# Attention scores of a cross-attention and FFN block: eight kept weight tables in place of a product per batch

## Chip, cores and metric

One core of a Trainium2 chip runs the kernel. The metric is the device time in microseconds; the time before is the median of three runs.

## What is computed

For each of 32 batches, with x and a context c of 256 rows and 512 columns:

```
q = layernorm(x)
t, p, g = Wt c, Wp q, Wg c                     (256 x 512 each)
score[G] = 0.125 * sum over group G's 32 rows and all columns of p * g      (8 groups)
u = Wz[G] (score[G] * t[G]);  normalised over each group, * gamma + beta, + c
x1 = x + that
out = x1 + FFN(layernorm(x1)),  gate/up 512 -> 1408, silu(gate) * up, down 1408 -> 512
```

The three linear layers of the FFN round their inputs and weights to FP4 (E2M1) in blocks of 16 with a scale each. The score of a group is linear in the matrix c q' (256 x 256, here called the gram matrix): it is the sum over all its elements of gram times the table Wg[G]' Wp[G].

## The kernel before

A batch is two tiles of 128 rows (t = 2b and 2b + 1; j counts tiles). The FFN weights are quantised, turned and split into two fp16 parts once at the start; they stay in SBUF. Each engine has its own list of steps, written out by hand, with semaphores between them; the first two batches are interleaved with the weight work, and then a loop `body(i)` runs for i = 1 to 30 (the last one unrolled). In body i the FFN of tiles j = 2i and j + 1 runs, beside the attention of batch i + 1 and the loading and normalising of batch i + 2.

TensorE's order in a body: `gram(i + 1)` (24 fp16 products of 256 columns, line 500), three hidden groups of tile j (`hidden`, line 550: two spans of 512 columns and one of 384, 24 products each, gate and up in turn), between the first and the second `mixed` (line 512: four fp32 products, Wg times gram) and `u_rows` twice (line 527: twelve F32R products of 512 columns, the context times the folded value weights), then `group_means` and `group_spread` (lines 535, 541: small fp32 products with a matrix of group means), `output(j - 1)` (line 561, 33 fp16 products), three hidden groups of tile j + 1, and `output(j)`. A hidden group may start when the `gated` step that reads its PSUM pair two groups before is done (`h_done`), and an output product when the transposed h has landed (`h_turned`).

The chain of h for a tile: ScalarE's silu (line 964), VectorE's `gated` (1409), block maxima (`h_first`, 1205), scales (`h_scales`), division (`h_y`, 1184), ScalarE's `grain_h` (915), VectorE's `h_snap_add` (1193), `h_snap_back` (1197), `h_quant` in two halves (1201), ScalarE's `h_hi` (873), VectorE's `h_lo` (1349), then SP's transposing DMA `turn_h` (422). For the odd tile j - 1 the part from `h_snap_add` on runs at the start of the next body. x has the same chain with 512 columns (`x_first`, `x_y`, `x_add`, `x_back`, `x_quant`, `x_lo`), and `turn_x`.

The scores: ScalarE's `gram_copy` (834) brings gram to SBUF, scaled by row; TensorE's `mixed` multiplies it by Wg; VectorE's `sum_pg` (1239) multiplies by Wp and sums each row; `group_means` adds the rows of a group; `copy_group` (1245) and GpSimd's `columns` go on. GpSimd also makes the low parts of the context (`ctx_lo`, 1797) and of q (`q_lo`, 1802), x + c (`add_ctx`, 1786), and the powers of -1/2 (1771). Line 1208 is VectorE's scale step; lines 1470, 1473 (VectorE) and 1848, 1856 (GpSimd) round and scale the weights at the start, and lines 597, 614 and 639 are TensorE's work there: the transposes of the weights, the row of maxima, and the folding of the value weights.

```python
            def mixed(b):
                pe.wait_ge(gram_copied, HT * b + HT)
                at_least(pe, pg_summed, HT * b)
...
            def h_snap_add(j):
                dve.wait_ge(h_grain_done, j + 1)
```

## Time and profile before

| | us |
|---|---|
| three runs: lowest, median, highest | 1741.19, 1742.09, 1744.41 |
| profiled execution: span from its first to its last instruction | 1739.4 |
| TensorE busy in the span | 1682.5 |
| VectorE busy | 1518.6 |
| ScalarE, GpSimd busy | 825.6, 707.2 |

The profile gives the span of the profiled execution and no other time of it; the span leaves out what lies before the first and after the last instruction. It is 2.7 us under the median of the runs. PE is TensorE's matmul, PEld its weight load, DVE is VectorE, ACT is ScalarE, POOL is GpSimd, SP is SyncE. A row of a timeline merges like instructions that follow one another (x8: eight of them); its time runs from the start of the first to the end of the last, and what stands in brackets is the idle time ahead of it and what ended that. Matmul records overlap: the next one starts before the end of the one ahead.

### The profile page before, as it was taken

How to read it: one execution, taken by the hardware profiler on the slowest of the kernel's cores; microseconds unless marked ns; L12 is line 12 of the kernel's file. 1: busy time of each engine (PE TensorE's matmuls, PEld its weight loads, DVE VectorE, ACT ScalarE, POOL GpSimd, SP SyncE). 2: the span in 40 equal slices, each digit the busy share in tenths (PEclk: the TensorE clock that was granted, in tenths of full speed). 3: DMA queues.
4: the chain of work that ended last, by engine and by line, in shares of the span. 5: the costliest groups of instructions: out<-in, count | busy, mean ns of one | idle time of the engine just before them, and what ended most of it. 6: DMA issues, size and time to landing. Idle time of an engine off the chain costs nothing.

```text
span 1739.4 us, 27808 instructions
## 1 busy us (share of the span) xinstructions
PE 1682.5 (97%) x8723; PEld 922.4 (53%) x8723; DVE 1518.6 (87%) x2577; ACT 825.6 (47%) x1472; POOL 707.2 (41%) x879
## 2 busy tenths in 40 slices
PE   2789999999999999999999999999999999999999
PEld 1666555555555555555555555555555555555544
DVE  8987888889888888988888898888888988888887
ACT  3656545444445454444554444454544444545322
POOL 6865333334444333444433334443333444433310
PEclk9999999999999999999999999999999999999999
DMA  8123334334344434343434434333434444333321
GB/s 257 34 43 66 88 89 105 88 91 97 78 94 91 94 87 99 89 96 79 93 89 94 98 83 106 75 87 90 104 87 92 96 81 93 91 92 87 76 52 47
DMA packets 412150, 155.86 MB, mean 90 GB/s; under 512 B 383200, under 2 KB 384480, under 8 KB 412128
## 3 DMA queue, kind: packets, MB, share of 16 engines
q1 hardware_dynamic: 396352, 125.17, 33.7%
q10 hardware_dynamic: 15776, 30.41, 5.4%
q8 instruction: 12, 0.20, 0.0%
q14 instruction: 10, 0.08, 0.0%
HBM read 43.03 MB, written 16.78 MB: 34 GB/s over the span
## 4 chain that ended last, share of the span: by engine, by line
PE 94%; DVE 2%; ACT 2%; DMA 1%; issue 1%; POOL 0%; SPq 0%; DVEq 0%; ACTq 0%
PE pairs L550 52%; PE work L561 25%; PE work L500 5%; PE work L512 3%; PE ubank L527 2%; PE work L527 2%; PE pairs L605 1%; PE pairs L500 0%; PE pairs L597 0%; DMA hT_parts<-raw 0%; DMA raw<-in_L_ffn_w_gate 0%; DVE w_rinv L1205 0%; DVE x_in L1223 0%; PE pairs L607 0%; PE pairs L580 0%
## 5 line engine op out<-in xcount | busy, mean ns | idle before, releaser
L550 PE MATMUL pairs<-w_gate_hi,xT_parts 128*128 128x512 f16 (+1 forms) x1536 | 555.4, 362 | 1.8 <-DMA xT_parts<-raw 1.5
L550 PE MATMUL pairs<-w_up_hi,xT_parts 128*128 128x512 f16 (+1 forms) x1536 | 554.7, 361 | 0.0
L561 PE MATMUL work<-w_parts,hT_parts 128*128 128x512 f16 x2079 | 458.9, 379 | 0.9 <-DMA hT_parts<-raw 0.9
L561 PEld LDWEIGHTS work<-w_parts,hT_parts 128*128 128x128 f16 x2079 | 203.5, 99 | 236.1 <-issue 1.1
L550 PE MATMUL pairs<-w_up_lo,xT_parts 128*128 128x512 f16 (+1 forms) x768 | 277.5, 361 | 0.0
L550 PE MATMUL pairs<-w_gate_lo,xT_parts 128*128 128x512 f16 (+1 forms) x768 | 277.4, 361 | 0.0
L550 PEld LDWEIGHTS pairs<-w_gate_hi,xT_parts 128*128 128x128 f16 x1536 | 152.7, 99 | 163.2 <-issue 15.1
L550 PEld LDWEIGHTS pairs<-w_up_hi,xT_parts 128*128 128x128 f16 x1536 | 150.3, 98 | 146.5
L964 ACT ACTIVATE early<-pairs,w_unit 128x512 f32<-128x512 f32 (+1 forms) x192 | 124.9, 651 | 166.3 <-PE pairs L550 166.3
L873 ACT CAST raw<-hq 128x704 f16<-128x704 f32 x126 | 98.1, 779 | 179.5 <-DVE hq L1201 178.7
L1409 DVE SCALAR_TENSOR_TENSOR h<-pairs,w_unit,early 128x512 f32<-128x512 f32 (+1 forms) x192 | 135.0, 703 | 39.9 <-ACT early L964 34.6
L915 ACT ACTIVATE wm<-h 128x1408 bf16<-128x1408 f32 (+2 forms) x65 | 87.1, 1341 | 166.5 <-DVE h L1184 166.5
L1786 POOL TENSOR_TENSOR xc<-x_in,c_in 128x512 f32<-128x512 f32 x64 | 88.8, 1387 | 176.6 <-DVE x L1258 176.6
L1835 POOL TENSOR_TENSOR ln_rs<-ln_mv,eps_col 128x1 f32<-128x1 f32 x64 | 59.2, 925 | 215.3 <-DVE ln_mv L1266 215.3
L1810 POOL TENSOR_TENSOR att<-rowst,grp 128x2 f32<-128x2 f32 x32 | 14.0, 436 | 280.6 <-DVE grp L1245 280.6
L1201 DVE SCALAR_TENSOR_TENSOR hq<-h,h_unit 128x704 f32<-128x704 f32 (+1 forms) x129 | 111.1, 882 | 5.5
L550 PEld LDWEIGHTS pairs<-w_gate_lo,xT_parts 128*128 128x128 f16 x768 | 75.1, 98 | 77.1
L550 PEld LDWEIGHTS pairs<-w_up_lo,xT_parts 128*128 128x128 f16 x768 | 75.1, 98 | 77.0
L1349 DVE TENSOR_TENSOR raw<-hq,raw 128x704 f16<-128x704 f32 x126 | 109.3, 887 | 1.6
L1205 DVE TENSOR_REDUCE h_amax<-h 128x88 f32<-128x1408 f32 (+1 forms) x66 | 104.0, 1575 | 2.2
L1184 DVE SCALAR_TENSOR_TENSOR h<-h,h_rinv 128x1408 f32<-128x1408 f32 (+1 forms) x66 | 104.1, 1577 | 0.1
L1197 DVE SCALAR_TENSOR_TENSOR h<-wm,h 128x1408 f32<-128x1408 bf16 (+2 forms) x65 | 102.7, 1580 | 1.2
(193 smaller groups left out, 2803.6 us busy)
## 6 DMA issues: line engine op xcount, KB each, us to landing
out<-raw SPq DMA_DIRECT2D x64, 256.0 KB, 2.1
c_in<-in_ctx ACTq DMA_DIRECT2D x29, 512.0 KB, 3.8
x_in<-in_x ACTq DMA_DIRECT2D x29, 512.0 KB, 5.3
raw<-in_L_ffn_w_down SPq DMA_DIRECT2D x2, 1408.0 KB, 8.9
raw<-in_L_ffn_w_gate SPq DMA_DIRECT2D x2, 1280.0 KB, 8.3
w_parts<-in_L_ffn_w_up SPq DMA_DIRECT2D x2, 1280.0 KB, 9.4
x_in<-in_x SPq DMA_DIRECT2D x3, 512.0 KB, 3.7
c_in<-in_ctx SPq DMA_DIRECT2D x3, 512.0 KB, 4.7
```

The lines of the kernel that those rows point to most:

```text
L550: mm = pe.matmul(pairs[:, pair, n, 0:b - a], xT[s][part][:, k, :], w1[n][wpart][:, k, a:b], start=(k == 0 and part == 0 and wpart == 0), s ...
L561: mm = pe.matmul(obank[:, :], hT[part][:, k, :], w2[wpart][:, k, :], start=(k == 0 and part == 0 and wpart == 0), stop=(k == KH - 1 and pa ...
L873: nc.scalar.copy(hq_parts[:, 0, a:b], hq[:, a:b]).then_inc(h_hi_done, 1)
L915: nc.scalar.activation(m, y, ACT.Abs, scale=GRAIN).then_inc(done, 1)
L964: nc.scalar.activation(silu[:, (s + c) % 2, 0:b - a], pairs[:, pair_of(j, s, c), 0, 0:b - a], ACT.Silu, scale=w_unit[:, 0:1]).then_inc(sil ...
L1184: nc.vector.scalar_tensor_tensor(out=blocks(y), in0=blocks(src), scalar=SNAP_BELOW, in1=over_block(rinv), op0=ALU.mult, op1=ALU.mult).then ...
L1197: nc.vector.scalar_tensor_tensor(out=y, in0=m, scalar=GRAIN, in1=y, op0=ALU.max, op1=ALU.subtract).then_inc(done, 1)
L1201: nc.vector.scalar_tensor_tensor(out=blocks(q_out), in0=blocks(y), scalar=-factor, in1=over_block(scale), op0=ALU.mult, op1=ALU.mult).then ...
L1205: nc.vector.tensor_reduce(dst, blocks(src), AX_X, ALU.max, apply_absolute_value=True).then_inc(done, 1)
L1349: nc.vector.tensor_tensor(hq_parts[:, 1, a:b], hq[:, a:b], hq_parts[:, 0, a:b], ALU.subtract).then_inc(h_lo_done, 1)
L1409: nc.vector.scalar_tensor_tensor(out=h[:, a:b], in0=pairs[:, pair_of(j, s, c), 1, 0:b - a], scalar=w_unit[:, 1:2], in1=silu[:, (s + c) % 2 ...
L1786: nc.gpsimd.tensor_tensor(xc[:, s, :], x_in[:, s, :], c_in[:, s, :], ALU.add).then_inc(xc_ready, 1)
```

## The change

From batch 2 on the scores no longer go through `mixed` and `sum_pg`. At the start TensorE makes the eight tables Wg[G]' Wp[G] (128 x 512 each in SBUF), ScalarE copies them out of PSUM, and they wait in DRAM until the weight work frees their place. In each body GpSimd multiplies the gram copy by tables 0 to 5 (`product`) and ScalarE sums each product's rows (`sum_product`), with a ring of three buffers; VectorE multiplies and sums tables 6 and 7 in one step each (`fold_product`). `group_means` gets a second small product with a matrix of ones, and `own_att` picks each row's group. The scores are made one body ahead: `gram(i + 2)` and `gram_copy(i + 2)` stand at the end of body i. The F32R products of `u_rows` are put one by one behind each pair of fp16 products of the hidden group (j, 0, 1) (`hidden_and_u`). `group_means` moves behind the third hidden group and `group_spread` behind `output(j - 1)`. Steps of ScalarE, VectorE, GpSimd and SP change their order in the body, and body 1 is unrolled. Cut to its core:

```diff
+AW = HT * C
+pg_low = raw[:, 0, 0:5 * AW].rearrange("p (g n) -> p g n", g=5)
+pg_high = raw[:, 2, 2 * D:2 * D + 3 * AW].rearrange("p (g n) -> p g n", g=3)
+pg_dram = nc.dram_tensor("pg_kept", [P, G, AW], F32).ap()
+w_small_row = w_small_parts[:].rearrange("p a b -> p (a b)")
+products = [wgT[:].rearrange("p a b -> p (a b)"), w_small_row[:, 0:AW], w_small_row[:, AW:2 * AW],
+            raw[:, 1, H + D:H + D + AW]]
+RING = len(products) - 1
+SPLIT = 6
+OLD = 2
 first_hm = hT_parts[:, 0].rearrange("p k n -> p (k n)").bitcast(BF16)
...
 def gram_bank(b):
-    return pairs[:, 0, 0, :] if isinstance(b, int) and b < 2 else work[:, 0, :]
+    return pairs[:, 0, 0, :] if isinstance(b, int) and b < OLD else work[:, 1, :]
 def mixed_bank(b):
-    return pairs[:, 0, 1, :] if isinstance(b, int) and b < 2 else work[:, 1, :]
+    return pairs[:, 0, 1, :]
+def pg_weights(g):
+    return pg_low[:, g] if g < 5 else pg_high[:, g - 5]
+def pg_staged(g):
+    return x1[:, g, :] if g < 4 else (h, hq)[(g - 4) // 2][:, (g % 2) * AW:(g % 2) * AW + AW]
+def pg_bank(g):
+    return (pairs[:, 0, 0, :], pairs[:, 0, 1, :], work[:, 1, :], pairs[:, 1, 1, :])[g % 4]
+def sums_before(b):
+    return SPLIT * (b - OLD)
+def folds_before(b):
+    return (G - SPLIT) * (b - OLD)
 def u_bank(b, s):
-    return gram_bank(b) if s else ubank[:, :]
...
             sp.dma_start(part, raw_dram[m][:, r, n * rest:(n + 1) * rest]).then_inc(raw_loaded[f], 16)
+    def load_pg():
+        sp.wait_ge(pg_saved, 48)
+        sp.wait_ge(w_rest_done, ALL_SETS)
+        sp.dma_start(pg_low, pg_dram[:, 0:5, :]).then_inc(pg_loaded, 16)
+        sp.dma_start(pg_high, pg_dram[:, 5:G, :]).then_inc(pg_loaded, 16)
     def turn_q(b):
...
         j = HT * i
         turn_h(j - 1)
         turn_x(j + 1, 1)
+        turn_h(j)
         if ahead:
             turn_c(i + 2)
+            turn_q(i + 2)
+        if more:
+            turn_x(j + 2, 0)
         store(j - 1, 1)
-        turn_h(j)
-        if ahead:
-            turn_q(i + 2)
-        if more:
-            turn_x(j + 2, 0)
         store(j, 0)
-    with sp.Fori(1, NB - 2) as i:
+    body(1)
...
-            at_least(pe, w_ready, b)
-            at_least(pe, rowst_ready, HT * b)
+            u_first(b)
         else:
-            pe.wait_ge(gram_copied, HT * b + HT)
+            u_second(b)
         for k in range(HT):
             for wpart, part in PARTS:
-                mm = pe.matmul(u_bank(b, s), wuT[wpart][:, k, s * P:(s + 1) * P], c_wide[part][:, k, :],
-                               start=(k == 0 and wpart == 0 and part == 0), stop=(k == HT - 1 and wpart == 1))
-        mm.then_inc(u_done, 1)
+                u_part(b, s, k, wpart, part)
+    def pg_matrix(g0):
+        for s in range(HT):
+            for g in range(g0, g0 + P // CG):
+                if s == 0 and g >= 4:
+                    pe.wait_ge(pg_copied, g - 3)
+                a = g % 4 * CG
+                mm = pe.matmul(pg_bank(g)[:, s * C:(s + 1) * C], w_nat[a:a + CG, 1, g // 4, s * P:(s + 1) * P],
+                               wp[a:a + CG, g // 4, :], start=True, stop=True)
+                if s == HT - 1:
+                    mm.then_inc(pg_in_psum, 1)
     def group_means(b):
         pe.wait_ge(u_copied, HT * b + HT)
-        pe.wait_ge(pg_summed, HT * b + HT)
         pe.wait_ge(rowst_ready, HT * b + HT)
-        pe.matmul(ubank[:, 0:6], gmean[:, :], rowst[:].rearrange("p h n -> p (h n)"), start=True,
-                  stop=True).then_inc(grp_done, 1)
+        if isinstance(b, int) and b < OLD:
+            pe.wait_ge(pg_summed, HT * b + HT)
+            pe.matmul(ubank[:, 0:6], gmean[:, :], rowst[:].rearrange("p h n -> p (h n)"), start=True,
+                      stop=True).then_inc(grp_done, 1)
+            return
+        pe.wait_ge(product_summed, sums_before(b) + SPLIT)
+        pe.wait_ge(product_folded, folds_before(b) + G - SPLIT)
+        pe.matmul(ubank[:, 0:2 * HT], gmean[:, :], rowst[:, :, 1:3], start=True, stop=True)
+        pe.matmul(ubank[:, 8:8 + G], ones_all[:, :], att_part[:, :], start=True, stop=True).then_inc(grp_done, 1)
     def group_spread(b):
         pe.wait_ge(sq_steps, 2 * b + 2)
         pe.wait_ge(grp_copied, b + 1)
+        if not isinstance(b, int) or b >= OLD:
+            pe.wait_ge(own_picked, b - OLD + 1)
         pe.matmul(ubank[:, 6:8], gmean[:, :], att[:, 1, :], start=True, stop=True).then_inc(spread_done, 1)
     def hidden(j, s, c):
...
         mm.then_inc(gu_done, 1)
+    def hidden_and_u(j, s, c, b):
+        pair = pair_of(j, s, c)
+        first, last = SPANS[c]
+        u_first(b)
+        for k in range(KD):
+            if k == KD // 2:
+                u_second(b)
+            for part, wpart in PARTS:
+                for n in range(2):
+                    mm = pe.matmul(pairs[:, pair, n, 0:last - first], xT[s][part][:, k, :],
+                                   w1[n][wpart][:, k, first:last],
+                                   start=(k == 0 and part == 0 and wpart == 0), stop=(k == KD - 1 and part == 1))
+                if k == KD - 1 and part == 1:
+                    mm.then_inc(gu_done, 1)
+                u_part(b, k // HT, k % HT, part, wpart)
     def output(j):
...
     mm.then_inc(attw_in_psum, 1)
+    pg_matrix(0)
+    pg_matrix(4)
     pe.wait_ge(ones_made, 1)
     top_of_rows(0)
     spread_top(0)
+    pe.wait_ge(pg_copied, G)
     turn_weights(0)
     turn_weights(1)
...
     output(0)
+    gram(2)
     def body(i):
         more = not isinstance(i, int) or i + 1 < NB
+        ahead = not isinstance(i, int) or i + 2 < NB
         j = HT * i
-        if more:
-            gram(i + 1)
         pe.wait_ge(x_turned, 16 * (j) + 16)
         pe.wait_ge(h_done, GROUPS * (j - 1) + 2)
         hidden(j, 0, 0)
         if more:
-            mixed(i + 1)
-            u_rows(i + 1, 0)
-            u_rows(i + 1, 1)
-        pe.wait_ge(h_done, GROUPS * (j))
-        hidden(j, 0, 1)
-        if more:
-            group_means(i + 1)
+            pe.wait_ge(h_done, GROUPS * (j))
+            hidden_and_u(j, 0, 1, i + 1)
+        if not more:
+            hidden(j, 0, 1)
         pe.wait_ge(h_done, GROUPS * (j) + 1)
         hidden(j, 0, 2)
         if more:
+            group_means(i + 1)
+        output(j - 1)
+        if more:
             group_spread(i + 1)
-        output(j - 1)
         pe.wait_ge(x_turned, 16 * (j + 1) + 16)
         pe.wait_ge(h_done, GROUPS * (j) + 2)
         hidden(j + 1, 1, 0)
...
         pe.wait_ge(h_done, GROUPS * (j + 1) + 1)
         hidden(j + 1, 1, 2)
         output(j)
-    with pe.Fori(1, NB - 2) as i:
+        if ahead:
+            gram(i + 2)
+    body(1)
+    with pe.Fori(2, NB - 2) as i:
         body(i)
     body(NB - 2)
     pe.wait_ge(x_turned, 16 * (NT - 2) + 16)
...
         act.wait_ge(c_inv_done, b + 1)
-        at_least(act, mixed_done, b)
+        if isinstance(b, int) and b <= OLD:
+            at_least(act, mixed_done, b)
+        else:
+            act.wait_ge(product_made, sums_before(b))
+            act.wait_ge(product_folded, folds_before(b))
         for s in range(HT):
             nc.scalar.activation(gram_sb[:, s, :], gram_bank(b)[:, s * C:(s + 1) * C], ACT.Identity,
                                  scale=c_norm[:, 3, s:s + 1]).then_inc(gram_copied, 1)
+    def copy_pg(g):
+        act.wait_ge(pg_in_psum, g + 1)
+        nc.scalar.copy(pg_staged(g), pg_bank(g)).then_inc(pg_copied, 1)
+    def save_pg():
+        act.wait_ge(pg_copied, G)
+        nc.scalar.dma_start(pg_dram[:, 0:4, :], x1[:]).then_inc(pg_saved, 16)
+        for n, kept in enumerate((h, hq)):
+            nc.scalar.dma_start(pg_dram[:, 4 + 2 * n:6 + 2 * n, :],
+                                kept[:, 0:2 * AW].rearrange("p (g n) -> p g n", g=2)).then_inc(pg_saved, 16)
+    def sum_product(b, g):
+        act.wait_ge(product_made, sums_before(b) + g + 1)
+        act.wait_ge(grp_done, b)
+        nc.scalar.activation(products[g % RING], products[g % RING], ACT.Identity,
+                             accum_out=att_part[:, g:g + 1]).then_inc(product_summed, 1)
     def copy_u(b, s):
         act.wait_ge(u_done, HT * b + s + 1)
...
                                     (wzT, obank[:, 0:HT * P]), (wuT[0], pairs[:, 1, 0, :]))):
         act.wait_ge(attw_in_psum, n + 1)
         nc.scalar.copy(dst[:, :, :].rearrange("p a b -> p (a b)"), src).then_inc(attw_copied, 1)
+    for g in range(G):
+        copy_pg(g)
+    save_pg()
     act.wait_ge(consts_made, 1)
     ctx_square(0)
     act.wait_ge(attw_split, 1)
...
+    gram_copy(2)
     grain_h(1)
     def body(i):
         more = not isinstance(i, int) or i + 1 < NB
         ahead = not isinstance(i, int) or i + 2 < NB
         j = HT * i
+        if more:
+            sum_product(i + 1, 0)
         if ahead:
             load_ctx(i + 2)
+        if more:
+            sum_product(i + 1, 1)
+        if ahead:
             load_x(i + 2)
         if more:
-            gram_copy(i + 1)
+            sum_product(i + 1, 2)
+        silu_group(j, 0, 0)
+        if more:
+            sum_product(i + 1, 3)
+        h_hi(j - 1, 0)
+        if more:
+            sum_product(i + 1, 4)
+        h_hi(j - 1, 1)
+        grain_x(j + 1)
+        if more:
+            copy_u(i + 1, 0)
+            sum_product(i + 1, 5)
+            u_moments(i + 1, 0)
         if ahead:
             ctx_square(i + 2)
-        h_hi(j - 1, 0)
-        h_hi(j - 1, 1)
-        silu_group(j, 0, 0)
-        if more:
...
+        silu_group(j + 1, 1, 2)
+        if more:
+            x_hi(j + 2)
         if ahead:
-            q_hi(i + 2)
-        silu_group(j + 1, 1, 2)
-        if more:
-            grain_x(j + 2)
-            x_hi(j + 2)
+            gram_copy(i + 2)
         grain_h(j + 1)
-    with act.Fori(1, NB - 2) as i:
+    body(1)
+    with act.Fori(2, NB - 2) as i:
         body(i)
     body(NB - 2)
...
+    def fold_product(b, g):
+        dve.wait_ge(gram_copied, HT * b + HT)
+        dve.wait_ge(grp_done, b)
+        if isinstance(b, int) and b == OLD:
+            dve.wait_ge(pg_loaded, 32)
+        at_least(dve, product_folded, folds_before(b) + g - SPLIT)
+        nc.vector.scalar_tensor_tensor(out=products[RING], in0=gram_sb[:].rearrange("p h n -> p (h n)"),
+                                       scalar=1.0, in1=pg_weights(g), op0=ALU.mult, op1=ALU.mult,
+                                       accum_out=att_part[:, g:g + 1]).then_inc(product_folded, 1)
     def copy_group(b):
         dve.wait_ge(grp_done, b + 1)
         at_least(dve, aff_steps, 9 * b)
-        nc.vector.tensor_copy(grp[:].rearrange("p h n -> p (h n)"), ubank[:, 0:6]).then_inc(grp_copied, 1)
+        if isinstance(b, int) and b < OLD:
+            nc.vector.tensor_copy(grp[:].rearrange("p h n -> p (h n)"), ubank[:, 0:6]).then_inc(grp_copied, 1)
...
+    def own_att(b):
+        dve.wait_ge(grp_done, b + 1)
+        at_least(dve, aff_steps, 9 * b)
+        nc.vector.tensor_tensor(att_own[:, :, :], ubank[:, 8:8 + G].rearrange("p (h g) -> p h g", h=HT),
+                                own_group[:, :].unsqueeze(1).to_broadcast([P, HT, P // CG]),
+                                ALU.mult).then_inc(own_masked, 1)
+        dve.wait_ge(own_masked, b - OLD + 1)
+        nc.vector.tensor_reduce(grp[:, :, 0], att_own[:, :, :], AX_X, ALU.add).then_inc(own_picked, 1)
...
         normalise2(j + 1)
+        x_first(j + 1)
+        x_scales(j + 1)
         h_snap_add(j - 1)
         h_snap_back(j - 1)
         h_quant(j - 1, 0)
-        x_first(j + 1)
         h_quant(j - 1, 1)
-        if more:
-            sum_pg(i + 1, 0)
+        gated(j, 0, 0)
+        x_y(j + 1)
         h_lo(j - 1, 0)
-        x_scales(j + 1)
-        x_y(j + 1)
         if ahead:
             ln1_moments(i + 2, 0)
-            ctx_power(i + 2)
-        gated(j, 0, 0)
-        if more:
-            sum_pg(i + 1, 1)
-        h_lo(j - 1, 1)
         x_add(j + 1)
         x_back(j + 1)
+        h_lo(j - 1, 1)
+        x_quant(j + 1)
+        if more:
+            fold_product(i + 1, 6)
+            fold_product(i + 1, 7)
+        gated(j, 0, 1)
+        gated(j, 0, 2)
+        x_lo(j + 1)
         if more:
             copy_group(i + 1)
-        x_quant(j + 1)
-        x_lo(j + 1)
-        gated(j, 0, 1)
+        h_first(j)
+        if more:
+            own_att(i + 1)
+        h_scales(j, 0)
...
+    def product(b, g):
+        pool.wait_ge(gram_copied, HT * b + HT)
+        if isinstance(b, int) and b == OLD:
+            pool.wait_ge(pg_loaded, 32)
+            pool.wait_ge(mixed_done, OLD)
+        at_least(pool, product_summed, sums_before(b) + g + 1 - RING)
+        nc.gpsimd.tensor_tensor(products[g % RING], gram_sb[:].rearrange("p h n -> p (h n)"), pg_weights(g),
+                                ALU.mult).then_inc(product_made, 1)
     def columns(b):
         pool.wait_ge(grp_copied, b + 1)
+        if not isinstance(b, int) or b >= OLD:
+            pool.wait_ge(own_picked, b - OLD + 1)
...
     def body(i):
+        more = not isinstance(i, int) or i + 1 < NB
         ahead = not isinstance(i, int) or i + 2 < NB
         j = HT * i
+        if more:
+            product(i + 1, 0)
+            product(i + 1, 1)
+            product(i + 1, 2)
+            product(i + 1, 3)
+            product(i + 1, 4)
+            product(i + 1, 5)
+        columns(i + 1)
         if ahead:
             ctx_root(i + 2)
-        columns(i + 1)
-        if ahead:
-            ctx_lo(i + 2, 0)
         columns_affine(i + 1)
         if ahead:
-            ctx_lo(i + 2, 1)
-            add_ctx(i + 2, 0)
             ln1(i + 2)
         root2(j + 2)
         if ahead:
+            add_ctx(i + 2, 0)
             add_ctx(i + 2, 1)
+            ctx_lo(i + 2, 0)
```

VectorE's body goes on with `h_y`, `ln1_moments`, `ctx_power`, `h_units` and the chain of tile j; at its end `x_add`, `x_back` and `x_quant` of tile j + 2 stand ahead of the last `gated`, where they stood behind it. On SP, `turn_h(j)` and `turn_q` now stand ahead of the stores.

## Rows read from the trace of the kernel before

**Rows 1.** the profile page, busy time by engine and the chain that ended last

```profile
PE 1682.5 (97%) x8723; PEld 922.4 (53%) x8723; DVE 1518.6 (87%) x2577; ACT 825.6 (47%) x1472; POOL 707.2 (41%) x879
...
PE 94%; DVE 2%; ACT 2%; DMA 1%; issue 1%; POOL 0%; SPq 0%; DVEq 0%; ACTq 0%
```

**Rows 2.** one body: window, length, busy us by engine, clock, DMA share, GB/s

```profile
829.05:879.41 50.36, 50.36 (x260) 26.98 (x260) 44.47 (x79) 24.05 (x44) 19.98 (x26) 1.00 0.41 91
```

**Rows 3.** the timeline of TensorE in that body: start, us, engine, line, operation

```profile
834.24 1.89 PE L512 MATMUL work<-gram_sb,wgT 128*128 128x256 f32 x8
...
836.20 0.39 PE L527 MATMUL ubank<-c_lo,wuT_hi 128*128 128x512 f32 x1
...
838.77 0.39 PE L550 MATMUL pairs<-w_gate_hi,xT_parts 128*128 128x512 f16 x1
...
848.00 0.28 PE L541 MATMUL ubank<-att,gmean 128*128 128x2 f32 x2
848.14 7.28 PE L561 MATMUL work<-w_parts,hT_parts 128*128 128x512 f16 x33
...
855.42 14.26 PE pairs L550 x72
...
876.64 2.78 PE L500 MATMUL work<-qT,cT 128*128 128x256 f16 x24
```

**Rows 4.** the timeline of ScalarE around the body's start: grain, gram copies, first squaring

```profile
828.33 1.38 ACT L915 ACTIVATE wm<-h 128x1408 bf16<-128x1408 f32 x1 [3.30 <-DVE h L1184]
...
829.92 0.84 ACT L834 ACTIVATE gram_sb<-work,c_norm 128x256 f32<-128x256 f32 x2 [0.21 <-issue]
832.57 0.63 ACT L880 ACTIVATE c_parts<-c_in 128x512 f16<-128x512 f32 x1 [1.80 <-DMA c_in<-in_ctx]
```

**Rows 5.** the timeline of VectorE in the body's first part

```profile
830.51 1.62 DVE L1193 SCALAR_TENSOR_TENSOR h<-wm,h 128x1408 f32<-128x1408 bf16 x1
832.16 1.62 DVE L1197 SCALAR_TENSOR_TENSOR h<-wm,h 128x1408 f32<-128x1408 bf16 x1
833.93 0.89 DVE L1201 SCALAR_TENSOR_TENSOR hq<-h,h_unit 128x704 f32<-128x704 f32 x1
...
838.00 0.69 DVE L1184 SCALAR_TENSOR_TENSOR xn<-xn,x_rinv 128x512 f32<-128x512 f32 x1
...
839.61 0.75 DVE L1409 SCALAR_TENSOR_TENSOR h<-pairs,w_unit,early 128x512 f32<-128x512 f32 x1
...
840.61 0.89 DVE L1349 TENSOR_TENSOR raw<-hq,raw 128x704 f16<-128x704 f32 x1
```

**Rows 6.** DMA issues, 824 to 885 us: count, median us to landing

```profile
hT_parts<-raw SPq DMA_TRANSPOSE x2, 5.2
```

**Rows 7.** the timelines of GpSimd and VectorE where both work, three places

```profile
850.67 1.27 POOL L1797 TENSOR_TENSOR c_lo<-c_in,c_hi 128x512 fp32r<-128x512 f32 x1
...
851.12 0.88 DVE L1208 TENSOR_SCALAR h_scale<-h_amax 128x88 f32<-128x88 f32 x1
...
860.29 1.69 DVE L1201 SCALAR_TENSOR_TENSOR hq<-h,h_unit 128x704 f32<-128x704 f32 x2
...
860.39 1.35 POOL L1771 TENSOR_TENSOR ln_rs<-ln_rs,minus_half 128x2 f32<-128x2 f32 x1
...
34.30 2.58 POOL L1856 TENSOR_TENSOR raw<-raw,w_scale 128x1408 f32<-128x1408 f32 x1
...
34.89 3.47 DVE L1470 SCALAR_TENSOR_TENSOR work<-wm,raw 128x1408 f32<-128x1408 bf16 x1
```

**Rows 8.** the timeline of TensorE at the kernel's start

```profile
17.27 2.07 PE L639 MATMUL pairs<-wzT,early 128*128 128x128 f32 x8 [0.46 <-ACT wzT L977]
19.27 0.58 PE L614 MATMUL ubank<-ident,w_max 128*1 128x128 f32 x2
```

**Rows 9.** TensorE after an idle time; four us: busy, clock, DMA

```profile
75.03 1.09 PE L597 MATMUL pairs<-ident,raw 128*128 128x128 f32 x4 [4.52 <-ACT w_gate_lo L944]
...
74.00:78.00 4.00, 2.96 (x13) 0.50 0.00 0
```

118 lines of the change are left out of this document (78 added, 40 removed).

## Prediction

> **What bounds the kernel now.** I read the busy times and the chain first, then one body of the loop, then the waits inside it. TensorE is busy 97% of the span and holds 94% of the chain that ended last; VectorE is busy 87%, ScalarE 47%, GpSimd 41% [rows 1]. In one body (one batch, two tiles) TensorE is busy for all of the 50.36 us, VectorE for 44.47 us [rows 2]. So removing TensorE work pays only as long as nothing arrives late, and VectorE has 5.9 us to give. Thirty bodies are changed (i = 1 to 30). The span is 1739.4 us, 2.7 us under the median of the runs (1742.09); I add the changes of the span to the median. A measurement of this kernel can tell about 0.2% (3.5 us) from no change.
>
> **TensorE.** `mixed` goes: four fp32 products, eight matmul records from 834.24 on. The second F32R product starts at 836.20; one pitch of 0.234 us back, the eight lasted to 835.97, so 1.73 us, 0.216 us apart [rows 3]. `group_means` gains a product with ones, priced as the small one there is, 0.14 us from 848.00 to 848.14 [rows 3]. Eleven F32R products take from 836.20 to 838.77, 0.234 us each, twelve 2.8 us [rows 3]. No row shows them between fp16 products; the fp32 records 0.216 us apart would put the twelve at -0.2 us, and the same 0.02 us lost again at each return to fp16 would be +0.2 us. I take 0, being nearest to the row of the same operation. TensorE's own sum is 50.36 - 1.73 + 0.14 = 48.8 us: -47 us for thirty bodies, if nothing else happens.
> The Trainium skill (TensorE: Matmul & The Clock Gate, "Wait — 56ns, not 53.3ns?") gives 215.7 ns from start to start for back-to-back products of 512 columns and names no type; by it the interleaved twelve would cost 2.59 us, 0.2 us a body less, 7 us over thirty. The F32R records here are slower (0.234 us), so the sum leaves this out.
>
> **The ring that gets tight.** The output product of the odd tile waits for a chain that now starts at the end of `gram`. Call T the end of `gram` as the body begins (829.05 in [rows 2]). Before, `grain_h` (1.38 us) ran ahead of `gram_copy` (0.84 us) [rows 4]; after, `gram_copy(i + 2)` stands ahead of `grain_h(j + 1)` on ScalarE and waits for `gram`. So grain ends at T + 2.4 (0.2 for the tail of the last record, 0.84, 1.38), and VectorE's snap-add cannot start before; before it started at 830.51, T + 1.46 [rows 5]. VectorE then runs snap-add 1.65 and snap-back 1.77 (by their starts), and the rest by the durations of [rows 5] less the 0.08 by which a step starts before the one ahead reports its end: two quantisations at 0.81, `gated` 0.66, x_y 0.61, `h_lo` 0.81, moments 0.61 (512 wide, like x_y), x_add and x_back 0.72 each (with a wait), `h_lo` 0.89: 10.0 us, to T + 12.4. The transpose of h issues at once and lands 5.2 us later [rows 6]: T + 17.7. TensorE would reach that output product at T + 17.3 (72 records of three groups in 14.26 us make a 512-wide group 5.2 and the 384-wide one 3.9; F32R 2.8, means 0.28 [rows 3]). From there to the next T: output 7.1 (7.28 less the last record's overlap), spread 0.14, three groups 14.26, output 7.1, `gram` 2.75, together 31.4 us [rows 3]. So even undisturbed the ring lasts 49.1 us, and the gain is at most 1.26 us a body, 38 us in all.
>
> **The six products on GpSimd.** Each reads two 128x512 fp32 tiles, as `c_lo` does: 1.27 us [rows 7]. They become ready at T + 1.0, when `gram_copy` ends, and so run against exactly the two-input steps above. The rows say what that does. VectorE's scale step of only 88 columns took 0.88 us at 851.12, under the second `c_lo` (850.67 to 851.94), though a 512-wide one takes 0.69 [rows 5]. A 1408-wide VectorE step that began 0.6 us after a 2.58 us GpSimd step took 3.47 us where its like takes 1.62 us [rows 5]; and GpSimd's two-column power, asked for at 860.39 under a quantisation, took 1.35 us and got in between the two back-to-back quantisations [rows 7]. So each blocks the other, and a waiting product slips in after the VectorE step under way.
> The Trainium skill (SBUF — State Buffer, "Who interferes with whom") speaks against this change: a VectorE instruction with two SBUF inputs and a GpSimd instruction that reads SBUF lock each other out for a whole instruction. By that rule, the trace agrees (3.47 against 1.62 us).
> The blocked step of 3.47 us did its own 1.62 from 36.74 on, 0.14 before GpSimd's end at 36.88; so one product between two such steps holds VectorE for 1.27 less 0.14 us at either end, 1.0 us. Product 0 runs before the snap-add (free). Product 1 (T + 2.3 to 3.5) holds up snap-add 0.95; 2, 3 and 4 fall between snap-add, snap-back and the quantisations, 1.0 each; 5 runs beside `gated`, which reads PSUM and is not held up, and costs x_y 0.35. Sum 4.3 us. The sums on ScalarE (0.63 us and a read-out each, like a squaring, six: some 4.8 us) keep up with the ring of three buffers, and ScalarE has 26 us idle in a body [rows 2, 4]; I cost them at nothing. Bounds of the hold-up: 0 (they never meet; nothing in it can be a gain) and 6 (all six in full). I take 4.3, as all three rows show a full hold.
> So the transpose lands at T + 22.0, TensorE idles 4.7 us before the odd tile's output, and a body lasts 49.1 + 4.3 = 53.4 us, 3.0 more than now: +91 us for thirty.
>
> **The rest.** Two folds on VectorE (0.75 each: a 512-wide step of 0.69 and a short read-out, estimated) and `own_att` (two small steps, 0.3) replace two 256-wide sums, together +0.9 us; they stand behind `h_lo` and hold `group_means` until T + 18.9, inside the wait above: 0, but 1.6 us a body if the ring were not there. Other moved steps of VectorE (x_add, x_back, x_quant of the next tile ahead of the last `gated`) free about 2.4 us at the body's end, in front of a wait for grain: 0. On SP, `turn_q` goes ahead of a store and `turn_h(j)` ahead of `turn_c`; `load_pg` waits for all weights with `turn_c(2)` behind it: 0, at most +5 us once. `group_spread` now waits for the odd tile's output and ends at T + 29.3; VectorE's `variance` stands ahead of the even tile's snap-add and waits for it. From there snap-add and snap-back, residual, emit, moments, two quantisations and two `h_lo` take some 8.8 us, the transpose 5.2: it lands at T + 43.4, where TensorE reaches that output at T + 43.5: 0, but with nothing to spare, so up to +1 us a body from `c_lo`, `q_lo` and `xc`, which GpSimd now runs one behind the other.
> At the start sixteen fp32 products of 256 columns and eight copies stand ahead of `top_of_rows(0)` at 19.27 us, for which VectorE waits, and ahead of the first squaring and grain. An fp32 product of 256 columns takes 0.43 us at the full clock (two records, [rows 3]), twice that at 1.2 GHz, at which the first products ran (eight 128-column records in 2.07 us, [rows 8]): 7 to 14 us, later stages absorb 0 to 5. I take +10.
> Sum: 1742.1 + 91 + 10 = **1843 us**.
>
> **Rivals.** (a) *Clock.* A 4.7 us idle may cost more than itself: after TensorE stood still from 70.5 to 75.03 us the granted clock of 74 to 78 us was 0.50, the 1.2 GHz level [rows 9]. If it falls in most bodies, some 3.4 us of the output run at half speed, +1.7 us a body: 1843 + 51 = 1894. Against: `group_means` breaks the idle. (b) *The other side, faster.* The products do not hold VectorE up on the ring, because they start later or lose every turn. Place: between snap-add and `h_lo`; price: 4.3 us; it decides once the hold-up is under 1.2 us a body. Then 49.1 us a body: 1742 - 38 + 10 = 1714, and 1705 if the transposes land a little earlier and TensorE's 48.8 us count. For it: in the body read, the long GpSimd steps held VectorE up by only 0.7 us [rows 7]. (c) *No change:* hold-up near 1 us, 50.1 us a body, the start eats the rest: 1744. (d) *TensorE gains nothing since VectorE is the bound:* 44.5 + 0.9 + 4.3 + 0.5 = 50.2 us a body, if the ring is met earlier than I reckon: 1747. (e) *It does not do what it says:* the interleaving costs time, each F32R product once more its 0.234 us, 2.8 us; with (b) that is 51.9 us a body, 1798.
>
> **Numbers.** Forecast 0.49; (a) 0.13; (b) 0.26; (c) 0.05; (d) and (e) 0.07. The forecast's own range, hold-up 2 to 5 us and start 5 to 15, is 1770 to 1880. The range for 8 in 10, 1706 to 1895, takes in most of (b), since 0.26 cannot be left out, and the lower half of (a). Faster by over 0.2%: 0.26; within: 0.05; slower: 0.69 (the forecast, (a), (d) and (e)).
>
> **What the changed profile would show.** Right: TensorE idle some 4 to 5 us a body before the odd tile's output, released by the transpose of h; snap and quantisation steps of the odd tile at 2.6 and 1.8 us where they now take 1.62 and 0.89; products well over 1.27 us; grain directly behind `gram_copy`; the first hidden products some 10 us later. Wrong: bodies under 50 us, the snap steps still at 1.62 us, or TensorE waiting in `group_means` or `gram` instead.

## The result, and the profile after

The changed kernel takes **2178.5 us** (median of 4 runs, 2177.4 to 2178.7) where the kernel before takes 1742.0 us (4 runs, 1741.2 to 1744.4): a ratio of 1.2505 (95% interval 1.2487 to 1.2523), 436.5 us slower. The forecast was slower too, 1843 us, but with a range that ended at 1895 us. The profiled execution spans 2175.6 us.

The page: busy times, then the chain that ended last. They answer to [rows 1].

```profile
PE 1777.2 (82%) x8575; PEld 898.1 (41%) x8575; DVE 1754.5 (81%) x2637; ACT 924.5 (42%) x1840; POOL 1045.8 (48%) x1065
...
DVE 28%; PE 25%; DMA 15%; issue 12%; ACT 9%; POOL 6%; SPq 3%; DVEq 1%; ACTq 0%; POOLq 0%
```

No engine is busy for more than 82% of the span, and the chain, which was 94% TensorE, now goes round through every engine and the DMA queues: that is what a ring of waits looks like. TensorE does fewer products and is still busy for 95 us more, so it ran slower as well. One body of the loop, in the columns of [rows 2]:

```profile
1024.37:1088.80 64.43, 52.91 (x252) 25.74 (x252) 52.28 (x81) 27.18 (x55) 31.06 (x32) 0.95 0.31 71
```

64.4 us in place of 50.36. The same body on TensorE's timeline (columns as in [rows 3]):

```profile
1024.37 4.21 PE L549 MATMUL work<-qT,cT 128*128 128x256 f16 x24 [5.32 <-DMA qT<-q_parts]
...
1033.84 0.58 PE L580 MATMUL ubank<-c_hi,wuT_hi 128*128 128x512 f32 x1
...
1034.52 0.58 PE L580 MATMUL ubank<-c_lo,wuT_hi 128*128 128x512 f32 x1
...
1047.96 0.38 PE L617 MATMUL ubank<-rowst,gmean 128*128 128x4 f32 x2 [2.13 <-ACT rowst L982]
...
1050.51 8.98 PE L662 MATMUL work<-w_parts,hT_parts 128*128 128x512 f16 x33 [1.94 <-DMA hT_parts<-raw]
1059.33 0.28 PE L625 MATMUL ubank<-att,gmean 128*128 128x2 f32 x2
...
1088.98 1.24 PE L549 MATMUL work<-qT,cT 128*128 128x256 f16 x5 [5.31 <-DMA qT<-q_parts]
```

T, the end of `gram`, is 1028.6. Two places lose time. Ahead of the odd tile's output TensorE waits twice (2.13 and 1.94 us), 4.1 us where 4.7 were forecast. The first of these waits ends with ScalarE's moments of u, 0.5 us after the last fold, which the forecast had as its end. And ahead of `gram` it waits 5.3 us for the transposed q, where nothing was forecast. In both the work behind the wait is slower: the output 8.98 us against 7.28, `gram` 4.21 against 2.78 [rows 3]. (The last row above is cut off by the window that I asked for; the whole `gram` takes 4.33 us there.) The stretches of 2 us around the output show why (window; length and busy us by engine; the number behind POOL is the granted clock):

```profile
1048.00:1050.00 2.00, 0.57 (x4) 0.48 (x4) 1.73 (x3) 1.22 (x3) 0.00 (x0) 1.00 1.06 200
1050.00:1052.00 2.00, 1.49 (x6) 0.58 (x7) 1.97 (x6) 0.00 (x0) 0.00 (x0) 0.80 0.29 59
1052.00:1054.00 2.00, 2.00 (x6) 0.72 (x5) 1.98 (x6) 0.00 (x0) 1.78 (x7) 0.50 0.39 72
```

At 0.50 TensorE runs at the 1.2 GHz level. Now the two legs between those products. First leg, T to the output: ScalarE's copy and grain, VectorE's snap steps, GpSimd's products beside them, SP's transpose (timelines of the four engines in turn):

```profile
1028.75 0.84 ACT L945 ACTIVATE gram_sb<-work,c_norm 128x256 f32<-128x256 f32 x2 [9.76 <-PE work L549]
1029.48 1.38 ACT L1045 ACTIVATE wm<-h 128x1408 bf16<-128x1408 f32 x1
...
1030.89 1.64 DVE L1341 SCALAR_TENSOR_TENSOR h<-wm,h 128x1408 f32<-128x1408 bf16 x1 [3.72 <-ACT wm L1045]
1032.56 2.57 DVE L1345 SCALAR_TENSOR_TENSOR h<-wm,h 128x1408 f32<-128x1408 bf16 x1
1035.28 3.63 DVE L1349 SCALAR_TENSOR_TENSOR hq<-h,h_unit 128x704 f32<-128x704 f32 x2
...
1031.01 5.26 POOL L1990 TENSOR_TENSOR w_small_parts<-gram_sb,raw 128x512 f32<-128x512 f32 x2
...
1045.29 3.32 SPq L469 DMA_TRANSPOSE hT_parts<-raw  x1
```

Second leg, from the spread to the next `gram`, as the chain that ended last lists it (start, us, what):

```profile
1059.98 1.42 POOL att L2011
1061.47 1.59 POOL att L2013
...
1071.64 1.52 DVE x L1432
1074.26 2.18 DVE x_in L1371 x2
...
1080.53 1.23 ACT c_parts L1033 x2
1081.84 2.06 SPq L455
1084.11 4.64 DMA qT<-q_parts
1088.98 3.16 PE work L549 x14
```

The two-column steps of GpSimd that follow `variance` take 1.42 and 1.59 us under VectorE's snap steps. In the kernel before no snap step ran beside them, and they took 0.20 and 0.19 (GpSimd's timeline):
```profile
848.63 0.20 POOL L1821 TENSOR_TENSOR att<-att 128x2 f32<-128x2 f32 x1 [0.76 <-DVE att L1251]
```
At the end of the leg `ctx_fit_lo` (ScalarE, 1080.53) stands late in ScalarE's order, `turn_c` waits for it, and `turn_q` stands behind `turn_c` on SP's queue.

**Three pieces make a body.** In each timeline I read how long it lasts from T to the end of the spread (A), from there to the start of the next `gram` (B), and `gram` itself (C). I read eight to eleven bodies per kernel, between 700 and 1300 us; where they differ, both ends stand. These are worked out from starts and lengths of the `gram` and spread records, like those above.

| kernel | A | B | C | body | time, us |
|---|---|---|---|---|---|
| before | 19.2 | 28.4 | 2.8 | 50.3 | 1742.0 |
| after | 31.0 to 31.4 | 29.3 to 29.4 | 4.2 to 4.4 | 64.6 to 65.1 | 2178.5 |

In the kernel before, B is TensorE's own work: output, three groups, output, 28.4 us by [rows 3], and nothing waits for q, which lands 27.1 us after `variance` (timelines of VectorE and SP in the kernel before, then its DMA issues from 824 to 885 us with the median landing):

```profile
848.32 0.16 DVE L1251 TENSOR_TENSOR att<-ubank,grp 128x2 f32<-128x2 f32 x1 [0.43 <-PE ubank L541]
...
871.10 1.94 SPq L401 DMA_TRANSPOSE qT<-q_parts  x1
```

```profile
qT<-q_parts SPq DMA_TRANSPOSE x1, 4.3
```

After the change one of those outputs lies in A, ahead of the spread. TensorE's own work in B is then only 21.4 us, but B stays at 29.4, because from the variance to q in TensorE's reach it takes that long. Output and q chain used to run side by side; now they run one behind the other.

### The profile page after: what moved, and what is told of

It reads as the page before. It is cut to its first block, busy times and chain, and to the rows that moved or that the text cites. A ratio compares the mean times of both kernels' runs of the same rounds, so it can differ in the third digit from the quotient of the medians.

```text
span 2175.6 us, 28776 instructions
## 1 busy us (share of the span) xinstructions
PE 1777.2 (82%) x8575; PEld 898.1 (41%) x8575; DVE 1754.5 (81%) x2637; ACT 924.5 (42%) x1840; POOL 1045.8 (48%) x1065
## 4 chain that ended last, share of the span: by engine, by line
DVE 28%; PE 25%; DMA 15%; issue 12%; ACT 9%; POOL 6%; SPq 3%; DVEq 1%; ACTq 0%; POOLq 0%
PE work L662 14%; DMA hT_parts<-raw 7%; DMA qT<-q_parts 6%; PE work L549 6%; DVE hq L1349 4%; DVE raw L1523 4%; DVE h L1345 4%; DVE x_in L1371 3%; SPq L455 3%; PE pairs L634 2%; DVE h L1341 2%; DVE x L1432 2%; POOL att L2013 2%; POOL att L2011 2%; DVE xn L1332 2%
## 5 line engine op out<-in xcount | busy, mean ns | idle before, releaser
L662 PE MATMUL work<-w_parts,hT_parts 128*128 128x512 f16 x2079 | 516.6, 412 | 72.4 <-DMA hT_parts<-raw 72.4
L634 PE MATMUL pairs<-w_gate_hi,xT_parts 128*128 128x512 f16 (+1 forms) x1296 | 464.4, 359 | 52.1 <-DVE h L1583 51.0
L634 PE MATMUL pairs<-w_up_hi,xT_parts 128*128 128x512 f16 (+1 forms) x1296 | 463.8, 358 | 0.0
L1990 POOL TENSOR_TENSOR w_small_parts<-gram_sb,raw 128x512 f32<-128x512 f32 x120 | 266.7, 2241 | 0.0
L549 PE MATMUL work<-qT,cT 128*128 128x256 f16 x720 | 126.9, 357 | 155.9 <-DMA qT<-q_parts 148.0
L1990 POOL TENSOR_TENSOR wgT<-gram_sb,raw 128x512 f32<-128x512 f32 x60 | 95.9, 1598 | 226.0 <-ACT gram_sb L945 226.0
L2025 POOL TENSOR_TENSOR ln_rs<-ln_mv,eps_col 128x1 f32<-128x1 f32 x64 | 32.5, 508 | 293.8 <-DVE ln_mv L1440 293.8
L549 PEld LDWEIGHTS work<-qT,cT 128*128 128x128 f16 x720 | 89.5, 128 | 199.7 <-issue 170.5
L1349 DVE SCALAR_TENSOR_TENSOR hq<-h,h_unit 128x704 f32<-128x704 f32 (+1 forms) x129 | 166.3, 1327 | 4.4
L989 ACT ACTIVATE v_sb<-u_sb,att 128x512 f32<-128x512 f32 x64 | 51.6, 807 | 269.7 <-POOL att L2021 268.5
L945 ACT ACTIVATE gram_sb<-work,c_norm 128x256 f32<-128x256 f32 x60 | 25.1, 470 | 296.7 <-PE work L549 296.7
L1432 DVE TENSOR_TENSOR x<-v_sb,xc 128x512 f32 (+1 forms) x64 | 74.1, 1158 | 81.8 <-ACT v_sb L989 81.8
```

The source lines that it names most:

```text
L549: mm = pe.matmul(dst[:, s * C:(s + 1) * C].rearrange("p (h n) -> p h n", n=P), cT[:, s, part, k, :], qT[:, :, qpart, k, :], start=(k == 0 ...
L634: mm = pe.matmul(pairs[:, pair, n, 0:b - a], xT[s][part][:, k, :], w1[n][wpart][:, k, a:b], start=(k == 0 and part == 0 and wpart == 0), s ...
L662: mm = pe.matmul(obank[:, :], hT[part][:, k, :], w2[wpart][:, k, :], start=(k == 0 and part == 0 and wpart == 0), stop=(k == KH - 1 and pa ...
L1349: nc.vector.scalar_tensor_tensor(out=blocks(q_out), in0=blocks(y), scalar=-factor, in1=over_block(scale), op0=ALU.mult, op1=ALU.mult).then ...
L1432: nc.vector.tensor_tensor(x1[:, t % 4, :], v_sb[:, :], xc[:, s, :], ALU.add).then_inc(x1_ready, 1)
L1990: nc.gpsimd.tensor_tensor(products[g % RING], gram_sb[:].rearrange("p h n -> p (h n)"), pg_weights(g), ALU.mult).then_inc(product_made, 1)
```

## The experiments

Two theories. **Series:** the two moved orders, `group_spread` behind the odd output and the context chain moved back, put the h leg and the q leg in series. **Hold-up:** GpSimd's six products and VectorE's snap steps block each other for longer than the 4.3 us that I had priced. A third, **clock**, says that most of it is TensorE at 1.2 GHz.

**Products cut to 2 of 512 columns** (e_tiny).
```
-  tensor_tensor(products[g % RING], gram_sb, pg_weights(g), mult)
+  tensor_tensor(products[g % RING][:, 0:2], gram_sb[:, 0:2], pg_weights(g)[:, 0:2], mult)
```

Expected of e_tiny:

> The changed kernel, each of GpSimd's six products a body cut from 512 columns to 2 (it leaves out nearly all of the products' work, so the scores are not the reference's); every step, wait and order stays. Lock theory (GpSimd's products hold up VectorE, and all of the loss follows from that): the snap and quantisation steps fall back to 1.62 and 0.89 us, and a body falls from 64.8 to under 50 us, some 1745. Series theory (since group_spread stands behind the odd tile's output, the chain of h and the chain of the attention run one after the other in every body, 29 us from spread to the next gram): the h leg shortens by 4.3 us and the clock's 2 us come back, the rest stays, a body of some 57 us, 1950. Clock theory alone: 2178 - 150 = 2030.

Measured 2009.5 us, 169 less and nearer to the series theory, though 60 us above its number. A falls to 25.1; B stays at 29.4 to 29.5, and C is 4.1 to 5.3, so `gram` still runs at the low clock, which the series theory's 1950 us had back at full. Hold-up alone is refuted: without the products' reading 267 us are still lost. VectorE's snap steps are back to the lengths of before [rows 5], and TensorE waits for q as long as ever:
```profile
1017.65 1.63 DVE L1341 SCALAR_TENSOR_TENSOR h<-wm,h 128x1408 f32<-128x1408 bf16 x1 [4.83 <-ACT wm L1045]
1019.31 1.65 DVE L1345 SCALAR_TENSOR_TENSOR h<-wm,h 128x1408 f32<-128x1408 bf16 x1
...
1010.04 5.30 PE L549 MATMUL work<-qT,cT 128*128 128x256 f16 x24 [5.31 <-DMA qT<-q_parts]
```

**grain_h ahead of gram_copy** (e_grain), then with the cut products too (e_gt).
```
-  gram_copy(i + 2)
   grain_h(j + 1)
+  gram_copy(i + 2)
```

Expected of e_grain:

> The changed kernel, with grain_h of the odd tile ahead of gram_copy on ScalarE, nothing else. Series theory: snap-add of the odd tile can start 3 to 4 us earlier, before gram ends, and the h leg shortens by 3 to 5 us a body: 2050, at most 2090. Lock theory alone: the same six products still hold up VectorE somewhere in the body, under 1 us a body gained: 2150 or more.

Expected of e_gt:

> The changed kernel with both: GpSimd's products cut to 2 columns (leaves out nearly all of their work) and grain_h ahead of gram_copy. Each alone took 120 to 170 us off. If both act on the one leg from gram to the odd tile's output, that leg is no longer the later one (TensorE's own work and the step to variance are) and together they give little more than the better one: 1985 to 2010. If they act on different legs they add: 1890.

2057.4 us and 2007.3 us. A becomes 26.3 to 27.1 in the first (28.3 in one body, where the clock fell in the output), 24.8 to 25.1 in the second, where TensorE's own work sets it (14.26 us of groups, 2.8 of u, 7.28 of output). The two savings lie on one stretch and don't add.

**group_spread back ahead of the odd output** (e_spread).
```
+  group_spread(i + 1)
   output(j - 1)
-  group_spread(i + 1)
```

Expected of e_spread:

> The changed kernel, with group_spread put back ahead of output(j - 1) on TensorE, nothing else. Series theory: variance comes some 7 us earlier, the output product some 2 us later, so a body shortens by 5 to 7 us: about 2000, and TensorE's wait for the transposed q falls from 5 to under 2 us. Lock theory alone: VectorE's work and hold-ups are unchanged, within 1%: 2160 to 2190.

2160.4 us, 18 less: a miss of 160 us for the series theory as I had put it.
```profile
1043.73 0.56 PE L625 MATMUL ubank<-att,gmean 128*128 128x2 f32 x2 [4.36 <-POOL att L2003]
1044.15 2.29 PE L662 MATMUL work<-w_parts,hT_parts 128*128 128x512 f16 x5
```
`own_att` stands behind `h_first` on VectorE, GpSimd's columns wait for it, and so TensorE stands 4.36 us in front of the spread with the output behind it. The whole output (9.5 to 10.2 us at the low clock) then falls into B, 34.8 to 35.5 us. And q stays tied to the output. On VectorE `normalise1` stands behind the `gated` of the hidden group that TensorE begins after the output, as in the kernel before, and behind the even tile's `h_lo`. That now waits 3.34 us for ScalarE's `h_hi`, which the change has put behind the `silu` of that same hidden group (timelines of ScalarE and VectorE):
```profile
1059.59 0.69 ACT L1094 ACTIVATE early<-pairs,w_unit 128x512 f32<-128x512 f32 x1 [4.84 <-PE pairs L634]
...
1060.98 1.69 DVE L1523 TENSOR_TENSOR raw<-hq,raw 128x704 f16<-128x704 f32 x2 [3.34 <-ACT raw L1003]
```
Moving only the spread ahead of the whole output gains little. No run moved that `silu` by itself.

**All eight folds on VectorE** (e_vec: `SPLIT = 0`, no products on GpSimd, no sums on ScalarE).

Expected of e_vec:

> The changed kernel with all eight tables on VectorE (fold_product at the place of the two, 0.62 us each), no products on GpSimd and no sums on ScalarE. Lock theory: hold-ups go, VectorE gets 3.7 us more work a body, about 1850. Series theory: the h leg is as short as without products, but the group means come 3.7 us later, ahead of the output: a body of 57 to 59 us, 1950 to 2010.

2074.9 us: above both. A 26.6, B 29.5 to 29.6, C 5.3: all of `gram` at the low clock, 2.5 us a body more than at the full one. Over thirty bodies that is 75 us; the time lies 65 us above the series theory's 2010. No product meets a snap step, and B is still the same: again not hold-up.

**TensorE kept busy in the wait for q** (e_warm: 18 fp16 products that nothing reads, ahead of `gram`).

Expected of e_warm:

> The changed kernel with eighteen more fp16 products of 512 columns ahead of gram at the end of a body (3.9 us at the full clock, into the bank that gram then overwrites), inside TensorE's 5.3 us wait for the transposed q. If the fallen clock costs what the rows show (gram 4.2 to 5.3 us in place of 2.75, and the hidden products behind it), a body shortens by 1.5 to 2.5 us: 2100 to 2135, and the mean granted clock rises above 0.96. If the clock costs nothing on the ring: 2178, or up to 2190 if the added products run past the wait.

2142.1 us, 36 less, 7 us short of the range expected. `gram` runs at the full clock and B is unchanged, so the clock at `gram` costs its 1.4 us and does not make q late. The output keeps the low clock here (8.7 to 10.2 us). Over both places the longer products of the changed kernel make 3.1 to 3.7 us a body, an estimate of some 100 of the 436 us; no run took the low clock away in both at once with the orders as they are.
```profile
1009.27 2.79 PE L549 MATMUL work<-qT,cT 128*128 128x256 f16 x24 [1.40 <-DMA qT<-q_parts]
```

**The context chain at its earlier places** (e_ctx), in short:
```
ScalarE: ctx_square behind grain_x, ctx_fit and ctx_hi behind x_hi, ctx_fit_lo behind grain_h
GpSimd:  ctx_root ahead of columns, ctx_lo ahead of columns_affine
VectorE: ctx_power ahead of gated(j, 0, 1)
SP:      turn_c(i + 2) ahead of turn_h(j)
```

Expected of e_ctx:

> The changed kernel with the chain of the context (square, root, power, fit, low part, turn_c) back near its old, earlier places on ScalarE, VectorE, GpSimd and SP, so that behind variance only the chain of q is left ahead of gram. Series theory: turn_q need not wait for turn_c and c_lo does not stand ahead of q_lo, 3 to 5 us a body less: 2030 to 2090. If the context's place does not matter: 2160 to 2190.

2003.9 us, 175 less, the largest single part and 26 us below the range expected. B falls from 29.4 to 24.5 or 24.6 and C to 2.8, 6.3 us together, and `gram` waits half a microsecond; A is 30.8 to 32.5. (The row is cut off by its window.)
```profile
1068.03 2.14 PE L550 MATMUL work<-qT,cT 128*128 128x256 f16 x18 [0.52 <-DMA qT<-q_parts]
```

The moves were made on four engines at once, and no run tells them apart.

**The same with grain_h first** (e_cg).

Expected of e_cg:

> The changed kernel with the context chain put back to its earlier places and grain_h issued ahead of gram_copy, nothing left out. Each alone gave 174.6 and 121.1 us. In the context run the chain of a body still passed through gram_copy, grain, the snap steps, the odd output and then variance, so by the theory of two legs in series the grain's saving is made on the same loop and most of it adds: 1890 to 1940 us. If the context chain's run had already left another bound (VectorE, or the GpSimd products), the two don't add: 1980 to 2010 us.

2021.6 us: a miss, 18 us slower than without. TensorE's wait in `group_means`, for ScalarE's moments, is 3.1 us here and 2.6 in e_ctx; what makes the moments late I did not test.

**The spread inside the odd output.** To loosen both ends of the knot, `group_spread` goes between the fourth and fifth of the output's eleven steps, and `own_att` next to `copy_group` ahead of `h_first`.
```
   for k in range(KH):
+      if k == 4: group_spread(i + 1)
...
   copy_group(i + 1)
+  own_att(i + 1)
   h_first(j)
-  own_att(i + 1)
```
Alone (e_mid), with the context chain (e_cm), with context chain and grain (e_cgs), and that with the products cut to 2 columns (e_cgst):

Expected of e_mid:

> The changed kernel with group_spread between the fourth and fifth step of the odd output, and copy_group with own_att ahead of h_first on VectorE; the context chain and grain_h stay where the change has them. Nothing is left out. Theory of series: variance comes about 5 us earlier in each body and everything behind it with it: 1990 to 2060 us. Rival (only the context chain's place matters, the spread's does not, as the run with the spread ahead of the whole output suggested): above 2130 us.

Expected of e_cm:

> The changed kernel with the context chain put back and group_spread inside the odd output, with grain_h behind gram_copy as in the change. Beside the run of all three (1930 us) it prices grain_h's place. If gram_copy's 0.84 us ahead of grain_h lies on the loop in every body: 1945 to 1965 us. If the loop no longer runs through it (VectorE is busy nine tenths): 1920 to 1940 us.

Expected of e_cgs:

> As the run before it, and group_spread stands between the fourth and fifth step of the odd output (where the kernel before let it run beside), with copy_group and own_att both ahead of h_first on VectorE, so that the variance no longer waits for the whole output. Nothing is left out. Theory of series: the two legs stand beside each other again, the loop loses the rest of the output behind the spread (4 to 5 us a body) and what is left is TensorE's own work at the clock granted: 1800 to 1890 us. Rival (the tables' work on VectorE and GpSimd sets the time whatever the order): above 1900 us, no gain over the run before it.

Expected of e_cgst:

> As the run before it, and each GpSimd product covers 2 of its 512 columns (the scores are left out in that part). It shows what the products' hold-up of VectorE is worth once the two legs are no longer in series. My forecast priced that hold-up at 4.3 us a body on the ring through grain and snap steps. By it: 1740 to 1790 us, 80 to 120 us below the run before it. If the hold-up is covered there: within 20 us of the run before it.

| kernel | A | B | C | body | time, us |
|---|---|---|---|---|---|
| e_mid | 26.9 to 27.5 | 30.5 to 31.0 | 4.3 to 5.3 | 62.2 to 63.2 | 2107.9 |
| e_cm | 26.5 to 27.6 | 26.5 | 2.8 | 55.8 to 56.9 | 1926.2 |
| e_cgs | 26.5 to 27.9 | 25.8 to 26.7 | 2.8 | 56.0 to 57.3 | 1930.2 |
| e_cgst | 20.7 to 20.8 | 29.3 to 29.6 | 2.8 | 52.9 to 53.1 | 1824.3 |

e_mid missed its range by 48 us and saved only 71 us: q still comes late (`gram` waits 4.3 us). The two orders together give 252 us (175 and 71 alone, 246 by addition), and the order of grain nothing, as the second expectation of e_cm has it. e_cgs ended 40 us above its range: TensorE is waiting less, but VectorE is now busy for nine tenths (272.3 of 300 us in e_cm). e_cgst is 106 us below e_cgs, as expected; its body is 3.1 to 4.4 us shorter, and its clock no longer falls (0.995 in the mean against 0.958). It ended 34 us above its range. What the products do to VectorE, by groups of its instructions from 700 to 1300 us (count, busy us, mean ns), first e_cm, then e_cgst:
```profile
L1350 DVE SCALAR_TENSOR_TENSOR hq<-h,h_unit 128x704 f32<-128x704 f32 x44 | 58.4, 1366 | 1.6
L1346 DVE SCALAR_TENSOR_TENSOR h<-wm,h 128x1408 f32<-128x1408 bf16 x21 | 43.3, 2062 | 0.3
L1342 DVE SCALAR_TENSOR_TENSOR h<-wm,h 128x1408 f32<-128x1408 bf16 x21 | 41.6, 1979 | 2.4 <-ACT wm L1046 2.4
```
```profile
L1350 DVE SCALAR_TENSOR_TENSOR hq<-h,h_unit 128x704 f32<-128x704 f32 x44 | 37.1, 885 | 1.6
L1346 DVE SCALAR_TENSOR_TENSOR h<-wm,h 128x1408 f32<-128x1408 bf16 x23 | 37.2, 1617 | 0.4
L1342 DVE SCALAR_TENSOR_TENSOR h<-wm,h 128x1408 f32<-128x1408 bf16 x23 | 36.6, 1592 | 2.4 <-ACT wm L1046 2.4
```
A body has two of each snap step and four quantisations: 2 x 0.39 + 2 x 0.45 + 4 x 0.48 = 3.6 us. `h_lo` (mean 1006 and 888 ns, four in a body) adds 0.5. The forecast said 4.3 with x_y among them.

**F32R products in a run, not between fp16 ones** (e_seq, the rest as e_cm).
```
-  hidden_and_u(j, 0, 1, i + 1)
+  u_rows(i + 1, 0); u_rows(i + 1, 1)
+  hidden(j, 0, 1)
```

Expected of e_seq:

> The changed kernel with the context chain put back and group_spread inside the odd output (1926 us), and the F32R products of u stand in one run ahead of the second hidden group as in the kernel before, not between its fp16 products. Nothing is left out. My forecast of the interleave: 0 us, within 0.2 us a body: 1920 to 1932 us. What the trace of the changed kernel shows (0.68 us for a step of two fp16 and one F32R product against 0.665 by the sum) would be 5 us: 1921. Rival (u earlier makes copies, moments and group_means earlier, and so the variance): 1890 to 1915 us.

1926.6 us (1926.1 to 1931.0) beside 1926.2: the interleaving makes no difference to the time. TensorE waits behind it in both kernels, for ScalarE's moments: 2.8 us in e_seq, 2.6 in e_cm. So the 0.2 us that the interleaved steps take longer are there, and the wait covers them.

**Products in TensorE's waits again**, in e_cm: six behind `group_means` (e_cmw), or twelve ahead of it (e_warm2).

Expected of e_cmw:

> The same kernel of 1926 us with six fp16 products of 512 columns more (into the bank that gram fills next) ahead of the odd output, in TensorE's wait of 1.6 us for the transposed h. There the first 12 products of the output took 4.25 us against 2.76 in the run whose clock did not fall. If the wait is what lowers the clock and TensorE's time is on the loop: up to 1.5 us a body less, 1885 to 1915 us. If VectorE sets the time there, the clock is not on the loop: 1920 to 1935 us.

Expected of e_warm2:

> The kernel of 1926 us (context chain back, group_spread inside the odd output) with twelve fp16 products of 512 columns more between the third hidden group and group_means, where TensorE stood still for 2.7 us and the clock then fell to the 1.2 GHz level: the odd output took 8.9 to 10.0 us against 7.28. Nothing is left out. If the lower clock is on the loop, the part of it ahead of the spread (about 1.4 us a body) is won: 1875 to 1895 us. If VectorE sets the time in between, 1915 to 1930 us.

1924.1 us (1912.4 to 1926.3) and 1907.8 us (1906.4 to 1909.7). In e_cmw the added products ran at the low clock themselves, since the clock had fallen in the wait of 2.66 us before them, for ScalarE's moments. Ahead of that wait they hold the clock in four of the ten bodies of e_warm2 that I read. TensorE's timelines, e_cmw and then such a body of e_warm2:
```profile
1050.18 0.58 PE L618 MATMUL ubank<-rowst,gmean 128*128 128x4 f32 x2 [2.66 <-ACT rowst L986]
...
1051.05 2.72 PE L883 MATMUL work<-w_parts 128*128 128x512 f16 x6
1053.57 4.22 PE L665 MATMUL work<-w_parts,hT_parts 128*128 128x512 f16 x12
```
```profile
1043.44 2.76 PE L665 MATMUL work<-w_parts,hT_parts 128*128 128x512 f16 x12 [1.60 <-DMA hT_parts<-raw]
```
In the other six the output still took 9.1 us. The gain, 18 us, is less than the 31 to 51 expected, and the bodies say why: with an output of 7.4 us or of 9.1, each lasts 55.7 us (in e_cm 55.7 and 56.9 in turn). So in e_warm2 the clock is no longer on the loop; that VectorE sets the time there (274.6 of 300 us busy) is an inference.

**The tables in the order of the kernel before**, all folds on VectorE, `group_means` behind the third hidden group, the spread inside the output (b_fold); the folds cut to 2 columns (b_foldt); eight products ahead of `group_means` (b_warm).

Expected of b_fold:

> The kernel before with the tables alone: scores by eight fold steps on VectorE, no mixed, no product on GpSimd, no sum on ScalarE, gram where it was, group_means behind the third hidden group and group_spread inside the odd tile's output product. TensorE has 48.8 us of work a body, VectorE 44.5 - 1.0 + 5.0 + 0.3 = 48.8. If the order and GpSimd's products are the cause of the loss and not the tables: 1730 to 1790. If the tables themselves cost it: above 1850.

Expected of b_foldt:

> The kernel with the tables in the order of the kernel before and all eight folds on VectorE (1875 us), and each fold covers 2 of its 512 columns (the scores are left out in that part). If the folds' reading time on VectorE is what the tables cost there, the kernel comes to the time of before plus the longer start, less what the shorter TensorE work gives: 1735 to 1775 us. If it is the order, the waits of group_means for the last fold, or the start: above 1820 us.

Expected of b_warm:

> The kernel with the tables in the order of the kernel before, all folds on VectorE (1875 us), with eight fp16 products of 512 columns more ahead of group_means, where TensorE waits 1.9 us for the last fold and the odd output then takes 9.1 us against 7.28. If the lower clock is on the loop: about 1.5 us a body less, 1825 to 1845 us. If VectorE (90% busy) sets the time: 1860 to 1880 us.

| kernel | A | B | C | body | time, us |
|---|---|---|---|---|---|
| b_fold | 24.0 | 27.9 | 2.8 | 54.7 | 1874.7 |
| b_foldt | 20.2 | 27.9 | 2.8 | 50.9 | 1770.1 |
| b_warm | 22.3 | 28.1 | 2.8 | 53.2 | 1835.7 |

b_fold met the second of its expectations: the tables cost time in this order too. One body in ten of b_fold kept the full clock and lasted 53.2 us. TensorE's wait and output in b_fold, then the output in b_warm:
```profile
1014.98 0.38 PE L615 MATMUL ubank<-rowst,gmean 128*128 128x4 f32 x2 [1.92 <-DVE raw L1378]
...
1015.61 4.25 PE L662 MATMUL work<-w_parts,hT_parts 128*128 128x512 f16 x12
```
```profile
1001.56 2.75 PE L662 MATMUL work<-w_parts,hT_parts 128*128 128x512 f16 x12
```
105 us of it go with the folds' reading, since b_foldt, within the first range of its expectation, takes 1770.1; 39 us (1.3 us a body) of these are the lower clock behind a wait of 1.9 us, by b_warm. b_foldt is still 28 us above the kernel before: a body of 50.8 to 50.9 us against 50.3 makes some 15 of them and the start some 7. In it TensorE waits 48 us, in 30 waits, for `gated`, which eats what the shorter TensorE work would give. b_warm, 5.5% slower than the kernel before (interval 5.3 to 5.7%), is the fastest kernel with whole tables among these runs; none beat the kernel before.

## Why the prediction was wrong

**TensorE's sum: right.** The `mixed` products went, `gram`'s neighbours kept their lengths, and the interleaved F32R step lasts 0.68 us (1033.84 to 1034.52) where two fp16 and one F32R product make 0.665: 0.2 us a body, which e_seq shows covered by the wait behind it.

**The ring up to the transpose: right.** Forecast: the last `h_lo` at T + 16.7, landing at T + 22.0. Measured: issued at 1045.29, T + 16.7, and the output starts at 1050.51, T + 21.9. The hold-up was forecast at 4.3 us a body and is 4.1 by the means of e_cm and e_cgst. But how it is spread was forecast wrong, and that the sum fits so well is in part luck. I had the snap-add and each later step held up once. By the starts in the body above snap-add was not held up at all, snap-back by 1.0, the two quantisations by 2.0 together, x_y by 0.3, and the first `h_lo`, which I had free, by 1.1; the cut of the products gives 106 us (3.5 us a body) once the orders are back, and 169 us (5.6) in the changed order, where the clock adds to it. The forecast's own range (1770 to 1880) has a slip at its upper end: a hold-up of 5 us and a start of 15 make 1869 us.

**"The rest": the step that failed.** I wrote that the spread ends at T + 29.3 (measured 31.0) and then followed only the even tile's h from there, "0, but with nothing to spare". The same VectorE order carries residual, `normalise1` and so q, for which `gram` waits. The trace of before had that length: 27.1 us from `variance` to the landing, 1.2 us before `gram` starts. With my own T + 29.3 that makes 29.3 + 27.1 + 2.8 = 59.2 us a body, 1742 + 30 x 8.84 + 10 = 2017 us. The body measured is 5.4 to 5.9 us longer still: 1.7 to 2.1 the output's lower clock in A, 2.3 the longer way to q in B, 1.4 to 1.6 `gram`'s lower clock. I priced the new order of the transposes on SP at 0 without following what they release, and the context chain's places on ScalarE, VectorE and GpSimd not at all; e_ctx prices all of these together at 175 us, and e_mid the spread's place at 71. On the even tile's own leg, "nothing to spare" was near: TensorE waits 0.62 us there for h, and 1.71 for `gated` before it, which I had at 0 too. `gram` waiting stood in my list of signs that would prove me wrong, and it should have been a rival with a price.

**Clock: right as a mechanism, its size and place short.** Rival (a) had 1.7 us a body behind the wait for h: the output is 1.7 to 2.1 us longer. It was a rival with 0.13; it happened in every body read, and in `gram` another 1.4 us. The reason against it, that `group_means` breaks the idle time, did not hold: it ran at 1047.96, between the two waits, and the clock stood at 0.50 from 1052 on all the same.

**Start:** +10 forecast. Its upper bound took the first products to run at 1.2 GHz from their lengths alone; the profile's granted clock reads 1.00 there (15 to 20 us), so that point is open. The first weight transposes begin at 43.60 instead of 36.93, +6.7 us (TensorE's timelines, the kernel before and then the changed one).
```profile
36.93 1.97 PE L597 MATMUL pairs<-ident,raw 128*128 128x128 f32 x8 [14.66 <-POOL raw L1856]
```
```profile
19.65 0.79 PE L602 MATMUL work<-wp,early 32*128 32x256 f32 x1
19.66 1.20 PE L602 MATMUL pairs<-wp,early 32*128 32x256 f32 x3
...
43.60 1.94 PE L698 MATMUL pairs<-ident,raw 128*128 128x128 f32 x8 [16.20 <-POOL raw L2046]
```
The records of the new products of 32 rows overlap (19.65 and 19.66), which I had not reckoned; that this is why it isn't 10 is an inference.

**The sum as the runs have it:** the two orders 252 us (2178.5 to 1926.2), the products' reading 102 to 106 us (1926.2 or 1930.2 to 1824.3, clock included), the start 7. The low clock is inside the first two, not beside them. The other 75 us of 1824.3 against 1742.0, 2.5 us a body, are open in part: TensorE there waits 1.9 us a body for `gated` ahead of the third hidden group (57 us in 30 waits), and the group means still stand behind folds and `copy_u`. No run took that wait away: it is there with the orders of the kernel before as well (b_foldt, 48 us). The two orders nearly add (175 + 71 = 246 of 252), but not all moves do: `grain_h` ahead of `gram_copy` was worth 121 us alone and cost 18 beside the context chain. So each of these is a price beside the other orders of this kernel, not a property of the move.

## What to carry to other kernels

When a step is moved behind a long one on an in-order engine, list everything that comes after it on every engine that waits for it, until each branch reaches the bounding engine again, and add up the longest branch from rows. A branch whose landing had 1.2 us to spare is on the path as soon as its head moves by more than that. Measure a loop as pieces between two events of the bounding engine (here A, B, C): legs that used to stand side by side show at once when they come to stand in series. And price a repair both alone and beside the others. The context chain and the spread added up; `grain_h`'s 121 us vanished beside the context chain; and the spread moved back by itself gave 18 us of the 178 expected, since q stayed tied to the output by way of VectorE and ScalarE.

## What the hardware showed that I had not expected

- A wait of 2 us can cost the clock, and need not. Behind 1.9 us of waiting, the output's first twelve products took 4.25 us against 2.75 (b_fold, b_warm), in nine of ten bodies of b_fold. In e_cgst TensorE waits as long in every body ahead of the third hidden group, and the mean granted clock is 0.995. The fall comes late: in the changed kernel the clock was 1.00 until 1050, 4 us into a stretch with little work, and 0.50 at 1052 to 1054, with the output, begun at 1050.51, already under way.
- Products that fill a wait helped here when they stood ahead of the first gap (twelve, 1907.8 us) and hardly when behind it (six, 1924.1, beside 1926.2 without), though the clock then fell in six of ten bodies even so.
- VectorE steps with two SBUF inputs and GpSimd steps hold each other up in both directions: a product (1.27 us for a like step in [rows 7]) took 2.24 us on average into two of the three ring buffers and 1.60 into the third; a two-column GpSimd step took 1.59 us in place of 0.19 in the path behind `variance`. The Trainium skill (SBUF — State Buffer, "Who interferes with whom") has it as a lock for a whole instruction, and this case's rows agree.
